# Five coefficient rows of a tile summed in PSUM by products with the identity, instead of by adds on GpSimd

## The chip, the cores and the metric

One core of one Trainium2 chip. The metric is device time in microseconds of one execution. The kernel computes in fp32 on TensorE (matrix products into PSUM), VectorE, ScalarE and GpSimd; SyncE issues the loads and stores. Each engine follows its own list of instructions in order, and they meet at semaphores.

## The reference, cut to what matters

```python
x = x + conv_block(_gn(x))          # 3x3 ternary convolution, 32 channels, 64x64, 16 images
x = x + omp_block(_gn(x))           # sparse coding of 4x4 patches
# omp_block: each patch of 512 numbers is a signal, the dictionary has 256 normalised atoms
for k in range(1, 6):               # five greedy steps for every patch
    index = argmax(|h| of the atoms not yet taken)
    # extend the Cholesky factor, solve for the k coefficients x_stack
    h = h_bar - x_stack @ G[I]
coeffs[b, I] = x_stack              # 5 nonzeros among 256
recon = D @ coeffs
```

For a tile of 128 patches, `coeffs` is a matrix of 128 x 256 with five nonzeros in a row. The kernel makes five matrices with one nonzero per row each, adds them, transposes the sum and multiplies it by the dictionary.

## The kernel before, in words

The 16 images are worked on in ROUNDS = 4 rounds r of IMG_R = 4 images; m counts the image slot. An image has two tiles of 128 patches; a round has two streams s = 0, 1 of TILES = 4 tiles each (two images). In round r the greedy steps k = 0 to 4 run on both streams. Beside them run the front of the next round f = r+1 (statistics, `norm_x`, `conv`, `norm_y`, `correlate`), and the back of the previous one, b = r-1 (coefficients, `reconstruct`, `out_back`, store). Nothing schedules this but the code: each engine's `body(r, front, behind)` calls the pieces in an order written by hand.

A greedy step: ScalarE takes |h| from PSUM into `score` (`scores`, L628). VectorE finds the eight largest and their places (`scan`, L906 and L912), drops those already taken (`select`), and extracts with masks the entries that it needs of the gathered Gram rows and of h (`extract`, `pick`, L964 and L967), then computes the coefficients (`solve`). GpSimd gathers the rows of the Gram matrix by indirect DMA (`gather`, L352), as soon as `select` has given the index. ScalarE builds diagonal matrices of the coefficient steps (`diags`, L637) and TensorE subtracts `diag` times `rows` from h (`update`, through the helper `mm`, L395, as all its ordinary products). VectorE waits for the score before `scan`.

The coefficients of image slot m: VectorE writes for each of its two tiles t five matrices of 128 x 256 into `picked[:, m % 2, t, j, :]`, j = 0 to 4 (`scatter`, L1054), and raises `picked_ready`. GpSimd adds matrices 1 to 4 onto matrix 0, four adds that wait for each other (`sum_picked`, L366), and raises `coef_ready`. TensorE transposes the sum in four blocks of 128 x 128 (`coef_transposes`, L483) into a PSUM tile of 128 x 512 (`back_ps0`, in the closing part `final_ps`, a view of `conv_ps`). ScalarE copies it with its sign turned to `coef_t` (`copy_coef`, L643). `reconstruct` adds, in two halves, x1 (by a product with the identity) and the dictionary times `coef_t`, and ScalarE evacuates each half (`out_back`, L650). `picked` has two places: `scatter` of slot m waits until slot m-2 is transposed.

Slot 0 of round r is scattered in the last selection of the round and slot 1 at its end; slots 2 and 3 have theirs in steps k = 1 and 2 of the next round. GpSimd adds slot 0 at the end of its round, and slots 1, 2 and 3 in the next, behind the gathers of (s, k) = (1, 0), (0, 2) and (0, 3). In TensorE's list `coef_transposes(b, 0)` and `reconstruct(b, 0)` stand between `correlate(r, 1)` and `update(r, 0, 0)`; `coef_transposes(b, 1)` behind `update(r, 0, 1)`; `reconstruct(b, 1)` behind `update(r, 1, 2)`; those of slot 2 behind `update(r, 0, 3)` and those of slot 3 behind `update(r, 1, 3)`, ahead of `correlate(f, 0)`. After the last round comes the closing part: the four images of round 3, one after the other. There VectorE itself adds the second tile of slots 2 and 3 (L1210).

On ScalarE, at the turn of a round: eight activations for the statistics of the next images (`x_statistics`), `scores(r, 1, 0)`, `copy_coef(b, 0)`, `root` (a square root that VectorE's `norm_params` awaits), `diags(r, 0, 0)`, `out_back(b, 0)`, `norm_x(f, 0)`, `scores(r, 0, 1)`, `norm_x(f, 1)`, `diags(r, 1, 0)`. Later `out_back(b, 1)` stands just before `diags(r, 0, 3)`.

Of the kernel before, what the change touches and what calls it, by code (L numbers as in the profile page):

```python
# [27 lines left out]
ALU = mybir.AluOpType  # L28
# [4 lines left out]
def build_program(nc, x_in, w_in, b_in, wc_in, bc_in, gate_in, dict_in, out):  # L33
    IMAGES, C, H, W = x_in.shape
    P = 128
# [5 lines left out]
    STEPS = 5  # L41
    IMG_R = 4
    ROUNDS = IMAGES // IMG_R
    TILES = 4
    CHUNKS = ATOMS // P
# [11 lines left out]
    with ctx:  # L57
# [3 lines left out]
        def sem(name):  # L61
            return ctx.enter_context(nc.semaphore(name))
# [4 lines left out]
        ident = sb("ident", [P, P])  # L67
# [53 lines left out]
        picked = sb("picked", [P, 2, 2, STEPS, ATOMS])  # L121
# [25 lines left out]
        final_ps = conv_ps[:, 0, :].rearrange("p (k n) -> p k n", k=CHUNKS)  # L147
# [47 lines left out]
        diag_ready = [sem(f"diag_ready{s}") for s in range(2)]  # L195
        h_read = [sem(f"h_read{s}") for s in range(2)]
        picked_ready = sem("picked_ready")
        coef_ready = sem("coef_ready")
        coef_ready_dve = sem("coef_ready_dve")
        coef_t_ps = sem("coef_t_ps")  # L200
        coef_t_done = sem("coef_t_done")
        recon_ps = sem("recon_ps")
# [4 lines left out]
        pool_step = sem("pool_step")  # L207
# [15 lines left out]
        def hold(eng, signal, value):  # L223

            eng.wait_ge(signal, value)
# [93 lines left out]
        @block.gpsimd  # L319
        def _(pool):  # L320
            n = 0

            def step(ins):
                nonlocal n
                n += 1
                ins.then_inc(pool_step, 1)
                pool.wait_ge(pool_step, n)

            step(nc.gpsimd.memset(ident[:, :], 0.0))
            step(nc.gpsimd.memset(same_channel[:, :], 0.0))  # L330
            step(nc.gpsimd.memset(center[:, :], 0.0))
            step(nc.gpsimd.memset(ones, 1.0))
            step(nc.gpsimd.iota(iota_i[:, :], pattern=[[1, ATOMS]], base=0, channel_multiplier=0))

            def put_ones(t, offset):

                step(nc.gpsimd.affine_select(out=t, in_=t, compare_op=ALU.not_equal, fill=1.0,
                                             base=-offset, pattern=[[1, t.shape[1]]], channel_multiplier=-1))

            put_ones(ident[:, :], 0)  # L340
            for q in range(1 - PATCH, PATCH):
                put_ones(same_channel[:, :], q * C)
            put_ones(center[:, 0:P // 2], 0)
            put_ones(center[:, P // 2:P], -C)
            step(nc.gpsimd.tensor_copy(iota_short[:, :], iota_i[:, :]))
            nc.gpsimd.tensor_copy(iota[:, :], iota_i[:, :]).then_inc(const_done, 1)

            def gather(r, s, k):

                hold(pool, idx_ready[s], (STEPS - 1) * r + k + 1)  # L350
                for t in range(TILES):
                    pool.indirect_dma_start(out=rows[s][:, k, t, :], out_offset=None, in_=gram_dram[:, :],  # L352
                                            in_offset=bass.IndirectOffsetOnAxis(ap=idx_u[s][:, k, t:t + 1], axis=0)
                                            ).then_inc(rows_in[s][t], 16)

            pool.wait_ge(gram_stored, 16)

            pool_base = n

            def sum_picked(r, m, tiles=(0, 1), left_out=0):  # L360


                for t in tiles:
                    hold(pool, picked_ready, 2 * (IMG_R * r + m) + t + 1)
                    for j in range(1, STEPS):
                        last = nc.gpsimd.tensor_tensor(picked[:, m % 2, t, 0, :], picked[:, m % 2, t, 0, :],  # L366
                                                       picked[:, m % 2, t, j, :], ALU.add)
                        if j < STEPS - 1:
                            count = pool_base + 2 * (STEPS - 2) * (IMG_R * r + m) + (STEPS - 2) * (t - left_out) + j
                            last.then_inc(pool_step, 1)  # L370
                            hold(pool, pool_step, count)
                    last.then_inc(coef_ready, 1)

            def body(r, behind):
                for k in range(STEPS - 1):
                    for s in range(2):
                        gather(r, s, k)

                        if behind and (s, k) in sums_after:
                            sum_picked(r - 1, sums_after[s, k])  # L380
                sum_picked(r, 0)

            sums_after = {(1, 0): 1, (0, 2): 2, (0, 3): 3}
            body(0, False)
            for r in range(1, ROUNDS):
                body(r, True)
            sum_picked(ROUNDS - 1, 1)
            sum_picked(ROUNDS - 1, 2, (0,))
            sum_picked(ROUNDS - 1, 3, (0,), 1)


        @block.tensor
        def _(pe):
# [16 lines left out]
            for c in range(PATCH):  # L410
                last = mm(back_ps[0][:, 0, :], ones, d_tmp[:, c, :], c == 0, c == PATCH - 1)
# [60 lines left out]
            def coef_transposes(r, m, dst=back_ps[0]):  # L472

                n = IMG_R * r + m
                by_dve = m - 1 if dst is final_ps and m >= 2 else 0
                pe.wait_ge(coef_ready, 2 * n + 2 - by_dve)
                if by_dve:
                    pe.wait_ge(coef_ready_dve, by_dve)
                if dst is back_ps[0]:
                    pe.wait_ge(y_done, 2 * n + 2)  # L480
                for k in range(CHUNKS):
                    for t in range(2):
                        last = nc.tensor.transpose(dst[:, k, t * P:(t + 1) * P],  # L483
                                                   picked[:, m % 2, t, 0, k * P:(k + 1) * P], ident[:, :])
                last.then_inc(coef_t_ps, 1)

            def reconstruct(r, m, final=False):
# [285 lines left out]
        def _(dve):  # L773
            v = nc.vector
            n = 0

            def step(ins):

                nonlocal n
                n += 1  # L780
                ins.then_inc(dve_step, 1)
                return n

            def after(count):

                dve.wait_ge(dve_step, count)
# [349 lines left out]
            for m in DVE_SQUARES:  # L1136
                dve.wait_ge(x1_done, 2 * m + 2)
                c = step(v.scalar_tensor_tensor(out=z[:, m, :], in0=x1[:, m, :], scalar=1.0, in1=x1[:, m, :],
                                                op0=ALU.mult, op1=ALU.mult, accum_out=sum_1[:, 2, m:m + 1]))
# [4 lines left out]
            for m in range(IMG_R):  # L1144
                c = step(v.tensor_scalar(z[:, m, :], x1[:, m, :], gn[:, 1, 8, m:m + 1], gn[:, 1, 9, m:m + 1],
                                         ALU.mult, ALU.add))
# [59 lines left out]

            for m in range(2, IMG_R):
                run(scatter(ROUNDS - 1, m))
                for j in range(1, STEPS):
                    c = step(v.tensor_tensor(picked[:, m % 2, 1, 0, :], picked[:, m % 2, 1, 0, :],  # L1210
                                             picked[:, m % 2, 1, j, :], ALU.add))
                    after(c)
                dve.sem_inc(coef_ready_dve, 1)


_INS = ['x', 'L0_conv_w', 'L0_conv_b', 'L0_conv_w_child', 'L0_conv_b_child', 'L0_conv_gate', 'L1_conv_dictionary']
# [18 lines left out]
```

## Time and profile before

| | |
|---|---|
| time, median of 3 runs | 603.63 us (602.96 to 605.72) |
| time of the profiled execution | 602.51 us |
| its span, first to last instruction | 600.7 us |
| TensorE (PE) busy | 457.0 us, 76%, 1778 instructions |
| VectorE (DVE) busy | 523.7 us, 87% |
| ScalarE (ACT) busy | 310.0 us, 52% |
| GpSimd (POOL) busy | 221.4 us, 37%: 127.5 in 128 gathers, 88.9 in 120 adds |
| chain that ended last | DVE 50%, PE 25%, issue 10%, ACT 6% |

The span is what the profiler saw between the first and the last instruction; the time of the execution is measured around it and is a little longer. PEld is TensorE's weight load, which runs beside its products. In a row of a timeline or a group, the last bracket tells how long the engine was idle before, and which instruction ended that.

### The profile page before, as it was taken

The numbers are of one execution on the slowest core, as the hardware profiler recorded it, in microseconds if no ns is written. First come the engines' busy times: TensorE is split into PE (matmuls) and PEld (weight loads), VectorE is DVE, ScalarE is ACT, GpSimd is POOL, SyncE is SP. The second block draws the span as 40 slices with busy tenths as digits, with TensorE's granted clock in tenths as the row PEclk, the third lists the DMA queues.
The fourth block names the chain that finished last, engine by engine and source line by source line (L and its number), as shares of the span: only waits on it lengthen the run. The fifth ranks groups of instructions, "written<-read, shape, count | busy, mean of one in ns | idle before, by whom it ended". The sixth has DMA issues, their size and how long they took to land.

```text
span 600.7 us, 7900 instructions
## 1 busy us (share of the span) xinstructions
PE 457.0 (76%) x1778; PEld 316.9 (53%) x1778; DVE 523.7 (87%) x2507; ACT 310.0 (52%) x682; POOL 221.4 (37%) x269
## 2 busy tenths in 40 slices
PE   0098949897659587889985797999983647896955
PEld 0034935455558343567873444677951535674643
DVE  4493579899999999999999999999999999889980
ACT  3544565785562757665576394658132433452212
POOL 3000045243004665471035656620347475404330
PEclk9999988898888899999998898989995877898868
DMA  6989024987000377651204341121113111211113
GB/s 105 173 114 151 17 60 96 161 124 118 5 1 6 101 130 140 121 102 34 53 19 100 74 97 44 37 71 37 35 47 95 41 50 50 71 35 36 35 35 70
DMA packets 108190, 43.41 MB, mean 72 GB/s; under 512 B 103408, under 2 KB 103920, under 8 KB 108144
## 3 DMA queue, kind: packets, MB, share of 16 engines
q1 hardware_dynamic: 102000, 26.13, 26.5%
q0 software_dynamic: 6144, 16.79, 10.8%
q8 instruction: 14, 0.23, 0.2%
q14 instruction: 32, 0.26, 0.1%
HBM read 34.24 MB, written 8.65 MB: 71 GB/s over the span
## 4 chain that ended last, share of the span: by engine, by line
DVE 50%; PE 25%; issue 10%; ACT 6%; SPq 5%; DMA 3%; POOL 0%; DVEq 0%
PE h L395 14%; DVE picked L1054 11%; DVE junk L967 9%; PE back_ps L395 7%; DVE junk L964 7%; DVE top_i L912 7%; DVE top L906 4%; PE conv_ps L395 4%; SPq L246 3%; ACT diag L637 1%; DVE mask L979 1%; SPq L253 1%; ACT xb L596 1%; ACT xa L596 1%; DMA xb<-in_x 1%
## 5 line engine op out<-in xcount | busy, mean ns | idle before, releaser
L395 PE MATMUL h<-rows,diag 128*128 128x256 f32 x640 | 173.2, 431 | 83.1 <-ACT diag L637 79.2
L352 POOL DMA_INDIRECT rows<-gram,idx_u x128 | 127.5, 996 | 213.5 <-DVEq L952 183.8
L395 PEld LDWEIGHTS h<-rows,diag 128*128 128x128 f32 x640 | 134.9, 217 | 124.2 <-issue 91.5
L366 POOL TENSOR_TENSOR picked<-picked 128x256 f32<-128x256 f32 x120 | 88.9, 744 | 144.9 <-DVEq L1058 137.7
L637 ACT ACTIVATE diag<-ident,dx 128x128 f32<-128x128 f32 x320 | 96.8, 388 | 69.9 <-DVEq L1041 69.8
L628 ACT ACTIVATE score<-h 128x512 f32<-128x512 f32 x80 | 47.2, 595 | 104.9 <-PE h L395 104.9
L1054 DVE TENSOR_SCALAR picked<-iota,idx_last,x_last 128x256 f32<-128x256 f32 x160 | 84.1, 561 | 1.5 <-DVE picked L1054 0.8
L967 DVE SCALAR_TENSOR_TENSOR junk<-mask,rows 128x256 bf16<-128x256 bf16 x224 | 82.4, 429 | 0.1
L906 DVE MAX8 top<-score 128x8 f32<-128x256 f32 x160 | 64.2, 413 | 13.3 <-ACT score L628 12.6
L395 PE MATMUL h<-d_sb,z 128*128 128x256 f32 x256 | 63.0, 407 | 9.0 <-DVEq L897 8.0
L395 PEld LDWEIGHTS h<-d_sb,z 128*128 128x128 f32 x256 | 61.0, 328 | 11.1 <-issue 8.9
L912 DVE FIND_INDEX8 top_i<-top,score 128x8 uint32<-128x256 f32 x160 | 64.9, 417 | 0.0
L395 PE MATMUL back_ps<-coef_t,d_t 128*128 128x256 f32 x256 | 64.1, 395 | 0.0
L395 PE MATMUL back_ps<-x,ident 128*128 128x256 f32 x128 | 63.1, 627 | 0.0
L395 PE MATMUL conv_ps<-xa,w_taps 128*64 128x512 f32 x128 | 62.2, 608 | 1.2 <-ACT x L606 0.8
L395 PEld LDWEIGHTS back_ps<-coef_t,d_t 128*128 128x128 f32 x256 | 51.8, 202 | 21.1 <-issue 14.2
L650 ACT ACTIVATE x<-back_ps 128x512 f32<-128x512 f32 x32 | 33.8, 1094 | 49.3 <-PE back_ps L395 49.3
L395 PE MATMUL conv_ps<-xb,w_taps 128*64 128x512 f32 x112 | 54.5, 610 | 0.0
L964 DVE SCALAR_TENSOR_TENSOR junk<-iota,idx_u,h 128x256 bf16<-128x256 f32 x96 | 44.2, 472 | 1.2 <-DVE idx_u L923 0.6
L964 DVE SCALAR_TENSOR_TENSOR junk<-iota,idx_u,rows 128x256 bf16<-128x256 f32 x96 | 43.4, 512 | 1.8 <-DVE picked L1054 0.7
L395 PEld LDWEIGHTS conv_ps<-xa,w_taps 128*64 128x64 f32 x128 | 16.6, 140 | 35.4 <-issue 33.3
L395 PEld LDWEIGHTS back_ps<-x,ident 128*128 128x128 f32 x128 | 25.6, 208 | 16.3 <-issue 14.6
(148 smaller groups left out, 577.9 us busy)
## 6 DMA issues: line engine op xcount, KB each, us to landing
xa<-in_x SPq DMA_DIRECT2D x64, 128.0 KB, 4.7
out<-x SPq DMA_DIRECT2D x64, 128.0 KB, 2.8
xb<-in_x SPq DMA_DIRECT2D x42, 128.0 KB
rows<-gram,idx_u POOLq DMA_INDIRECT x128, 2.9
xb<-in_x SPq DMA_DIRECT2D x14, 120.0 KB
rows<-in_x SPq DMA_DIRECT2D x6, 128.0 KB, 4.4
d_sb<-in_L_conv_dictionary SPq DMA_DIRECT2D x4, 128.0 KB, 4.0
gram<-coef_t SPq DMA_DIRECT2D x1, 256.0 KB, 2.2
```

The lines of the kernel that those rows point to most:

```text
L246: sp.dma_start(xa[channels(q), m, down:GR + down, 1:W + 1], rows_of(src, q)).then_inc(xa_loaded[m], 16)
L352: pool.indirect_dma_start(out=rows[s][:, k, t, :], out_offset=None, in_=gram_dram[:, :], in_offset=bass.IndirectOffsetOnAxis(ap=idx_u[s][: ...
L366: last = nc.gpsimd.tensor_tensor(picked[:, m % 2, t, 0, :], picked[:, m % 2, t, 0, :], picked[:, m % 2, t, j, :], ALU.add)
L395: return nc.tensor.matmul(dst, lhs, rhs, start=start, stop=stop, skip_group_check=skip)
L628: nc.scalar.activation(score[s][:, 2 * b:2 * b + 2, :], h[s][:, 2 * b:2 * b + 2, :], ACT.Abs).then_inc(score_ready[s], 1)
L637: last = nc.scalar.activation(diag[s][:, t, j, :], ident[:, :], ACT.Copy, scale=dx[s][:, t, j:j + 1])
L650: nc.scalar.activation(dst[:, 2 * half:2 * half + 2, :], back_ps[half][:, :, :], ACT.Copy).then_inc(y_done, 1)
L906: first.append(step(v.max(out=top[s][:, t, :], in_=score[s][:, t, :])))
L912: step(v.max_index(out=top_i[s][:, t, :], in_max=top[s][:, t, :], in_values=score[s][:, t, :]))
L964: c = step(v.scalar_tensor_tensor(out=place, in0=iota[:, :], scalar=idx_u[s][:, k, t:t + 1], in1=source, op0=ALU.is_equal, op1=ALU.mult, a ...
L967: c = step(v.scalar_tensor_tensor(out=place, in0=mask[:, t, :], scalar=1.0, in1=source, op0=ALU.mult, op1=ALU.mult, accum_out=dst))
L1054: c = step(v.tensor_scalar(picked[:, m % 2, t, j, :], iota[:, :], idx_last[m // 2][:, tile, j:j + 1], x_last[m // 2][:, tile, j:j + 1], AL ...
```

## The change

`sum_picked` and its calls go. `coef_transposes` multiplies each of the five matrices of a tile by the identity and lets PSUM accumulate, so that a block's sum comes out transposed; it waits for `picked_ready` of each tile. VectorE's adds in the closing part go as well. Nothing else is changed.

```diff
-            def sum_picked(r, m, tiles=(0, 1), left_out=0):
-                for t in tiles:
-                    hold(pool, picked_ready, 2 * (IMG_R * r + m) + t + 1)
-                    for j in range(1, STEPS):
-                        last = nc.gpsimd.tensor_tensor(picked[:, m % 2, t, 0, :], picked[:, m % 2, t, 0, :],
-                                                       picked[:, m % 2, t, j, :], ALU.add)
...
-                    last.then_inc(coef_ready, 1)
-
-            def body(r, behind):
+            for r in range(ROUNDS):
                 for k in range(STEPS - 1):
                     for s in range(2):
                         gather(r, s, k)
-
-                        if behind and (s, k) in sums_after:
-                            sum_picked(r - 1, sums_after[s, k])
-                sum_picked(r, 0)
...
             def coef_transposes(r, m, dst=back_ps[0]):
                 n = IMG_R * r + m
-                by_dve = m - 1 if dst is final_ps and m >= 2 else 0
-                pe.wait_ge(coef_ready, 2 * n + 2 - by_dve)
-                if by_dve:
-                    pe.wait_ge(coef_ready_dve, by_dve)
                 if dst is back_ps[0]:
                     pe.wait_ge(y_done, 2 * n + 2)
-                for k in range(CHUNKS):
-                    for t in range(2):
-                        last = nc.tensor.transpose(dst[:, k, t * P:(t + 1) * P],
-                                                   picked[:, m % 2, t, 0, k * P:(k + 1) * P], ident[:, :])
+                for t in range(2):
+                    pe.wait_ge(picked_ready, 2 * n + t + 1)
+                    for k in range(CHUNKS):
+                        for j in range(STEPS):
+                            last = mm(dst[:, k, t * P:(t + 1) * P], picked[:, m % 2, t, j, k * P:(k + 1) * P], ident[:, :],
+                                      t == 0 and k == 0 and j == 0, j == STEPS - 1, True)
                 last.then_inc(coef_t_ps, 1)
...
             for m in range(2, IMG_R):
                 run(scatter(ROUNDS - 1, m))
-                for j in range(1, STEPS):
-                    c = step(v.tensor_tensor(picked[:, m % 2, 1, 0, :], picked[:, m % 2, 1, 0, :],
-                                             picked[:, m % 2, 1, j, :], ALU.add))
-                    after(c)
-                dve.sem_inc(coef_ready_dve, 1)
```

On TensorE, from `update(1, 0, 3)` to `reconstruct(1, 0)` at the turn from round 1 to round 2, the order before (a row is a run of like products; `h<-rows,diag` is `update`, `back_ps<-ident,picked` is `coef_transposes`, the two kinds behind it `reconstruct`, `h<-d_sb,z` `correlate`):

```order
178 L395 MATMUL h<-rows,diag 128x256 x16
179 L483 MATMUL back_ps<-ident,picked 128x128 x4
180 L395 MATMUL back_ps<-x,ident 128x256 x2
181 L395 MATMUL back_ps<-coef_t,d_t 128x256 x4
182 L395 MATMUL back_ps<-x,ident 128x256 x2
183 L395 MATMUL back_ps<-coef_t,d_t 128x256 x4
184 L395 MATMUL h<-rows,diag 128x256 x16
185 L483 MATMUL back_ps<-ident,picked 128x128 x4
```

and with the change:

```order
178 L365 MATMUL h<-rows,diag 128x256 x16
179 L365 MATMUL back_ps<-ident,picked 128x128 x20
180 L365 MATMUL back_ps<-x,ident 128x256 x2
181 L365 MATMUL back_ps<-coef_t,d_t 128x256 x4
182 L365 MATMUL back_ps<-x,ident 128x256 x2
183 L365 MATMUL back_ps<-coef_t,d_t 128x256 x4
184 L365 MATMUL h<-rows,diag 128x256 x16
185 L365 MATMUL back_ps<-ident,picked 128x128 x20
```

Twenty ordinary products stand where four transposes stood, at all sixteen places, and no place has moved. On GpSimd, from the first round to the second, the order before is

```order
17 L352 DMA rows<-gram,idx_u 128x256 x32
18 L366 TENSOR_TENSOR picked<-picked 128x256 x8
19 L352 DMA rows<-gram,idx_u 128x256 x8
20 L366 TENSOR_TENSOR picked<-picked 128x256 x8
21 L352 DMA rows<-gram,idx_u 128x256 x12
22 L366 TENSOR_TENSOR picked<-picked 128x256 x8
```

and with the change all 128 gathers follow each other with nothing between:

```order
17 L350 DMA rows<-gram,idx_u 128x256 x128
```

## Rows read from the trace of the kernel before

**Rows 1.** The page, busy time and share of the span of each engine.
```profile
PE 457.0 (76%) x1778; PEld 316.9 (53%) x1778; DVE 523.7 (87%) x2507; ACT 310.0 (52%) x682; POOL 221.4 (37%) x269
```

**Rows 2.** The tile `picked`: instructions, duration ns min/median/max, first and last start.
```profile
L1054 DVE TENSOR_SCALAR picked<-iota,idx_last,x_last x160: 395/406/896, 169.5 to 582.2; 128x256 f32<-128x256 f32 x160
L366 POOL TENSOR_TENSOR picked<-picked x120: 721/727/994, 180.2 to 581.4; 128x256 f32<-128x256 f32 x120
L483 PEld LDWEIGHTS back_ps<-ident,picked x48: 140/141/225, 189.3 to 540.4; 128*128 128x128 f32 x48
```

**Rows 3.** Timeline, 184 to 190 us: start us, us, engine, line, operation.
```profile
184.04 3.14 POOL L366 TENSOR_TENSOR picked<-picked 128x256 f32<-128x256 f32 x4 [0.70 <-DVEq L1058]
184.06 3.60 DVE L1054 TENSOR_SCALAR picked<-iota,idx_last,x_last 128x256 f32<-128x256 f32 x5
...
187.81 1.71 DVE L1054 TENSOR_SCALAR picked<-iota,idx_last,x_last 128x256 f32<-128x256 f32 x5 [0.15 <-DVE picked L1054]
```

**Rows 4.** Stretches: from:to length, busy us of each engine, PEclk, DMA share.
```profile
197.11:320.91 123.80, 105.89 (x436) 73.08 (x435) 119.86 (x597) 78.75 (x174) 55.23 (x64) 0.97 0.43 85
320.91:445.02 124.11, 108.06 (x435) 75.22 (x434) 119.64 (x587) 70.19 (x157) 54.89 (x63) 0.94 0.24 59
445.02:547.85 102.83, 70.25 (x245) 51.20 (x244) 96.52 (x477) 41.91 (x106) 49.24 (x57) 0.82 0.21 56
547.85:594.43 46.58, 34.38 (x112) 24.02 (x112) 34.99 (x98) 10.71 (x12) 16.37 (x23) 0.82 0.20 46
```

**Rows 5.** Timeline of TensorE's products at slot 3 of round 0.
```profile
288.40 0.60 PE L483 MATMUL back_ps<-ident,picked 128*128 128x128 f32 x4
288.84 1.97 PE L395 MATMUL back_ps<-x,ident 128*128 128x256 f32 x4
290.63 1.91 PE L395 MATMUL back_ps<-coef_t,d_t 128*128 128x256 f32 x8
292.38 1.97 PE L395 MATMUL back_ps<-x,ident 128*128 128x256 f32 x4
...
295.92 7.63 PE L395 MATMUL h<-d_sb,z 128*128 128x256 f32 x32
```

**Rows 6.** Weight loads in the views of `w_taps` and `coef_t`, ns min/median/max.
```profile
L395 PEld LDWEIGHTS conv_ps<-xa,w_taps x128: 132/136/232, 33.0 to 375.1; 128*64 128x64 f32 x128
...
L395 PEld LDWEIGHTS back_ps<-coef_t,d_t x256: 187/190/333, 191.2 to 593.8; 128*128 128x128 f32 x128
```

**Rows 7.** Groups of VectorE's instructions, 452.82 to 459.30: busy us, mean ns.
```profile
L1054 DVE TENSOR_SCALAR picked<-iota,idx_last,x_last 128x256 f32<-128x256 f32 x5 | 3.6, 733 | 0.0
L964 DVE SCALAR_TENSOR_TENSOR junk<-iota,idx_u,rows 128x256 bf16<-128x256 f32 x2 | 1.9, 970 | 0.0
```

**Rows 8.** The page, a group of the extractions over the whole span.
```profile
L964 DVE SCALAR_TENSOR_TENSOR junk<-iota,idx_u,h 128x256 bf16<-128x256 f32 x96 | 44.2, 472 | 1.2 <-DVE idx_u L923 0.6
```

**Rows 9.** Timeline of TensorE, four places where it waits in rounds 1 and 2.
```profile
206.44 3.75 PE L395 MATMUL h<-rows,diag 128*128 128x256 f32 x8 [5.96 <-ACT diag L637]
...
267.01 4.34 PE L395 MATMUL h<-rows,diag 128*128 128x256 f32 x19 [2.17 <-ACT diag L637]
...
304.18 7.82 PE L395 MATMUL h<-d_sb,z 128*128 128x256 f32 x32 [0.64 <-DVEq L897]
312.97 0.39 PE L395 MATMUL conv_ps<-sum_x,same_channel 128*128 128x8 f32 x2 [0.97 <-ACT z L581]
```

**Rows 10.** The chain that ended last, at the second half of `out_back(0, 0)`.
```profile
198.42 1.12 ACT x L650
```

**Rows 11.** Timeline of VectorE, third tile of `scan(3, 0, 1)`.
```profile
450.85 0.43 DVE L906 MAX8 top<-score 128x8 f32<-128x256 f32 x1 [0.43 <-ACT score L628]
```

**Rows 12.** Timeline of TensorE, closing part: `coef_transposes` of slots 0 and 2.
```profile
553.45 1.12 PE L483 MATMUL conv_ps<-ident,picked 128*128 128x128 f32 x4 [5.61 <-POOL picked L366]
...
577.21 1.09 PE L483 MATMUL conv_ps<-ident,picked 128*128 128x128 f32 x4 [6.60 <-DVEq L1213]
```

More of the change, by code:

```diff
@@ L197, in build_program @@
         picked_ready = sem("picked_ready")
-        coef_ready = sem("coef_ready")
-        coef_ready_dve = sem("coef_ready_dve")
         coef_t_ps = sem("coef_t_ps")
@@ L356, in _ @@
             pool.wait_ge(gram_stored, 16)
-            pool_base = n
-            def sum_picked(r, m, tiles=(0, 1), left_out=0):
-                for t in tiles:
-                    hold(pool, picked_ready, 2 * (IMG_R * r + m) + t + 1)
-                    for j in range(1, STEPS):
-                        last = nc.gpsimd.tensor_tensor(picked[:, m % 2, t, 0, :], picked[:, m % 2, t, 0, :],
-                                                       picked[:, m % 2, t, j, :], ALU.add)
[L368 to L371, printed above, removed]
-                    last.then_inc(coef_ready, 1)
-            def body(r, behind):
+            for r in range(ROUNDS):
                 for k in range(STEPS - 1):
@@ L377, in body @@
                         gather(r, s, k)
-                        if behind and (s, k) in sums_after:
-                            sum_picked(r - 1, sums_after[s, k])
-                sum_picked(r, 0)
[L383 to L389, printed above, removed]
         @block.tensor
```

## The prediction

> **What bounds the kernel now.** I read the busy shares first [rows 1]: VectorE is busy 87% of the span, TensorE 76%, GpSimd 37%. GpSimd is far from full, so taking 88.9 us of adds from it buys nothing by itself; the question is whom those adds disturb, and whether TensorE has room for what replaces them. Second, the view of the tile `picked` [rows 2]: the scatter instruction of VectorE (L1054) has a median of 406 ns but a maximum of 896. The timeline shows when it is slow [rows 3]: while GpSimd adds, five scatters take 3.60 us (720 ns each); when it has stopped, the next five take 1.71 us. So the two engines shut each other out here. The Trainium skill (SBUF — State Buffer, section "SBUF: two separate sides") says that a VectorE instruction in a two-port mode and a GpSimd instruction hold one port pair exclusively, and the loser blocks; by that rule the trace agrees, 720 ns being about one add's 727 [rows 2].
>
> Third, the stretches. I cut the span at the ends of the three `reconstruct(b, 0)`, of the last `reconstruct` before the closing part and of the last of all: 197.11, 320.91, 445.02, 547.85, 594.43 [rows 4]. In the two stretches of a full round TensorE is busy 105.9 and 108.1 of 124 us, VectorE 119.9 and 119.6: VectorE leads, and TensorE follows with 16 to 18 us of room. That room is what the change spends.
>
> **Step 1, the price of a sum on TensorE.** Now four transposes per image start 0.44 us ahead of what follows, 110 ns each [rows 5]. After, an image takes 20 fp32 products of 128x128 by 128 columns. They aren't transposes, and every ordinary fp32 product shows as two records: `back_ps<-coef_t,d_t` has 4 in the program's order per half, 8 in the trace, at (292.38-290.63)/8 = 219 ns for 256 columns, hence 110 ns for 128 [rows 5]. Is the weight load hidden at that rate? A fp32 load of 64 columns takes 136 ns, of 128 columns 190 [rows 6]; 54 ns for 64 columns is some 107 ns of occupancy for 128, the rest fixed latency that overlaps, as it does for the transposes (loads of 141 ns at a pace of 110 [rows 2, 5]). So load and stream both need about 110 ns and run side by side: 40 records x 0.110 = **4.4 us an image, 3.96 more than now**. No row shows the form itself. The bounds: nothing can stream faster than a transpose's single record, 20 x 0.110 = 2.2 us; and with each load's full 190 ns exposed 40 x 0.190 = 7.6 us. I take 4.4, since its two halves each have a row.
>
> The Trainium skill (TensorE: Matmul & The Clock Gate, section "Terms") calls transpose mode four times faster for fp32. By that rule a product would be 440 ns, an image 8.8 us. The rows make the factor 2 (110 ns against two records of 110), so my sum goes by 2; the factor 4 speaks against this change and is kept as a rival.
>
> **Step 2, what leaves.** 120 GpSimd adds, and 8 adds of VectorE at the end. With them goes the lock-out. Beside the adds of image slot 1, VectorE in 452.82 to 459.30 shows five scatters at 733 ns (against 406) and two extractions at 970 (against 472) [rows 2, 7, 8]: 5x0.33 + 2x0.50 = 2.6 us, with small instructions 3.1. Slot 0 costs twice the 1.89 us that five scatters lose [rows 3], 3.7. For slots 2 and 3, where the adds lie mostly beside instructions that aren't slowed, I estimate half of slot 1's each, 1.5. That is some 10 us a round of VectorE's time, 30 in three rounds, and in the closing part some 13 (five tiles of slowed scatters at 1.89, and 8 adds of its own at about 0.45). It is a true saving of busy time, but it counts only where VectorE still leads.
>
> **Step 3, where it lands.** Against the profiled execution: span 600.7, its own time 602.51; the median of the runs shown is 603.63, 0.2% above it.
>
> - To the first `reconstruct(b, 0)`'s end: `correlate(r, 1)` starts when VectorE has read h, before the adds, so nothing comes earlier, and `coef_transposes(b, 0)` stands before `reconstruct`: **+3.9 us**. VectorE's early 3.6 us end in a wait: ScalarE must copy these coefficients before its square root of the statistics and before `out_back`, `norm_x` and the scores that VectorE wants next.
> - First full stretch, now 123.8. TensorE needs its 105.9 busy [rows 4], plus 4 x 3.96 = 15.8, plus idle time that no engine's spare time removes. First, after `reconstruct(b, 0)` ScalarE evacuates, scores, normalises and builds the diagonals before `update(r, 1, 0)`: 206.44-198.42 = 8.0 us [rows 9, 10], of which `update(r, 0, 0)`, 8 records of 0.219, fills 1.75: 6.3. Second, 2.2 us before `update(r, 0, 3)` [rows 9], whose diagonals queue on ScalarE behind `out_back(b, 1)`. Third, 1.6 us (0.64+0.97) at the end of the round, where ScalarE's eight statistics must finish before the sums. Together 131.8: **+8.0**. VectorE would need 124-10 = 114, so TensorE is now the bound.
> - Second full stretch, now 124.1: the same work at the same clock, without the statistics: 105.9+15.8+6.3+2.2 = 130.2, **+6.1**.
> - Last round, now 102.8, without convolutions: TensorE idles a third of it [rows 4]. The score that VectorE awaited at 450.85, 5.8 us after `reconstruct(b, 0)` [rows 11], comes 2.4 us after it (1.75 of update, 0.6 of score), since the gathered rows have long landed: -3.4. VectorE leads and saves 3.1+1.5. Then `coef_transposes(b, 2)` and `(b, 3)` stand in the path again, +7.9: **-0.1**. What slot 3 saves is lost in the wait for `out_back(b, 1)`, which queues before these diagonals on ScalarE.
> - Closing part, now 46.6, with TensorE idle 5.6 and 6.6 us, awaiting adds of GpSimd and of VectorE [rows 12], and the granted clock 0.82 [rows 4]. These waits vanish: the sums are now late themselves and the scatters early. Four times 4.4 + 7.08 (a `reconstruct`, 288.84 to 295.92 [rows 5]) = 45.9: **-0.7**.
>
> Sum +17.2: span 618, its time **620 us**, 2.8% slower. Everything that the adds cost VectorE is given back as waiting for TensorE, and the closing waits are filled by the new products.
>
> **The rivals.** (A) *The weight load isn't hidden.* At 190 ns a record an image costs 3.2 us more than forecast. Fifteen of the sixteen images lie on the path above (1, 4, 4, 2, 4), so +48: 668 us; with half the latency exposed, 647. By the skill's factor 4 (8.8 us an image, 4.4 more than forecast) +66: 686 us, with 0.03 of this rival's 0.15, for the rows speak for 2. For it: no row has 128 weight columns on 128 moving ones in fp32. Against: in the 256-column form the load is hidden entirely.
> (B) *The products are as cheap as transposes*, one record of 110 ns, 2.2 us an image: 15 x 2.2 = 33 us less than forecast, 587 us, faster than before. It decides at each `coef_transposes`; below about 3.3 us an image (17.2/15 = 1.15 under 4.4) the change is no slower. Against: all ordinary fp32 products come as two records. 0.08.
> (C) *VectorE stays the bound everywhere*, and TensorE's 144 idle us swallow the products: 603.6 less some 40 of lock-out, 563 us. For it: VectorE's 87%. Against: the full stretches leave TensorE 16 to 18 us, 10 of them in waits of TensorE for ScalarE for TensorE that products can't fill. 0.04.
> That the change doesn't do what it says is excluded by the order: 20 products for each 4 transposes, no add left on either engine.
>
> **How the numbers follow.** A measurement of this kernel can tell about 0.5% from no change. Forecast 0.68, its own range 607 to 632 (0.4 us an image on fifteen is 6 us; slow or full clock in three updates 5). Rival A 0.15, B 0.08, C 0.04, and 0.05 that the price lies so between B and mine that nothing shows. Slower 0.83, same 0.05, faster 0.12. The range takes in the half-exposed load at 647 and ends at 606; outside are B, C and the full rival A, about 0.2.
>
> **What would show it.** Right: the products at 110 ns a record, 640 of them; scatters all near 406 ns; VectorE busy near 480 us; the full stretches near 131 us with VectorE waiting for scores at the k=4 scans and at the first scan after `reconstruct(b, 0)`; no idle time of TensorE in the closing part. Wrong in size: a pace of 150 ns or more. Wrong in kind: VectorE still without gaps in the full rounds, or 320 records.

## The result, and the profile after

| | before | changed |
|---|---|---|
| median | 604.67 us (602.96 to 611.05, 4 runs) | 634.68 us (632.05 to 636.88, 4 runs) |
| profiled execution, its span | 602.51, 600.7 us | 633.46, 631.6 us |

The ratio is 1.047, 95% interval 1.039 to 1.056: **slower by 4.7%**, against 2.8% forecast (620 us, range 606 to 647). (The table of the kernel before had three runs; the fourth here is the 611.05.) The changed kernel took 625.2 us in a later set of runs, ratio 1.037 (1.033 to 1.040); the last experiments are about that difference.

The page of the changed kernel, busy times, the shares of the chain that ended last, and two groups (busy us, mean ns of one, idle before):

```profile
PE 517.2 (82%) x2354; PEld 383.3 (61%) x2354; DVE 478.4 (76%) x2499; ACT 312.3 (49%) x682; POOL 134.1 (21%) x149
...
PE 64%; DVE 12%; ACT 8%; issue 5%; SPq 5%; DMA 4%; DVEq 0%; ACTq 0%
...
L874 DVE MAX8 top<-score 128x8 f32<-128x256 f32 x160 | 64.5, 414 | 59.6 <-ACT score L596 58.6
...
L365 PE MATMUL back_ps<-ident,picked 128*128 128x128 f32 x480 | 55.7, 275 | 0.0
```

TensorE and VectorE have changed places [rows 1]: TensorE from 76 to 82%, VectorE from 87 to 76%, and TensorE holds 64% of the chain where it held 25%. VectorE, which before awaited scores for 12.6 us, now awaits them for 58.6.

The tile `picked` in the changed kernel (ns min/median/max, first and last start):

```profile
L365 PEld LDWEIGHTS back_ps<-ident,picked x480: 190/192/207, 190.9 to 571.8; 128*128 128x128 f32 x160
...
L1022 DVE TENSOR_SCALAR picked<-iota,idx_last,x_last x160: 382/407/416, 170.6 to 598.4; 128x256 f32<-128x256 f32 x160
```

No scatter takes 896 ns any more [rows 2]: the longest is 416. The weight load is indeed 190 ns long, as the row of `coef_t` promised [rows 6]. Whether it is hidden shows in TensorE's timeline at the place of [rows 5]:

```profile
298.19 4.63 PE L365 MATMUL back_ps<-ident,picked 128*128 128x128 f32 x40
302.66 1.97 PE L365 MATMUL back_ps<-x,ident 128*128 128x256 f32 x4
```

20 products are 40 records, and they take 302.66-298.19 = 4.47 us, 112 ns each, less than the load's 190: it is hidden. The stretches, cut as before at the ends of `reconstruct(b, 0)`, of the last `reconstruct` of the rounds and of the last of all (columns as in [rows 4]):

```profile
202.83:338.80 135.97, 123.17 (x581) 91.18 (x581) 111.54 (x602) 79.89 (x174) 33.03 (x34) 0.96 0.42 78
338.80:477.43 138.63, 125.39 (x580) 93.64 (x579) 108.54 (x584) 71.06 (x157) 35.17 (x35) 0.93 0.23 58
477.43:579.22 101.79, 78.50 (x355) 63.17 (x354) 88.68 (x467) 40.11 (x101) 24.56 (x24) 0.88 0.18 47
579.22:625.36 46.14, 46.13 (x257) 36.29 (x255) 16.44 (x77) 11.10 (x12) 0.00 (x0) 1.00 0.21 46
```

| change in us | start | first full | second full | last round | closing | sum |
|---|---|---|---|---|---|---|
| forecast | +3.9 | +8.0 | +6.1 | -0.1 | -0.7 | +17.2 |
| this execution | +5.7 | +12.2 | +14.5 | -1.0 | -0.4 | +31.0 |

The excess of 14 us sits in the two full stretches, 12.6 of it. What stands there that the forecast hadn't: first TensorE's wait before `update(1, 0, 2)`. The kernel before had one there as well, of 2.96 us (3.35 in the next round); the forecast didn't keep it:

```profile
239.77 5.42 PE L395 MATMUL h<-rows,diag 128*128 128x256 f32 x24 [2.96 <-ACT diag L637]
```

In the changed kernel, TensorE, and what ScalarE does meanwhile:

```profile
245.62 5.42 PE L365 MATMUL h<-rows,diag 128*128 128x256 f32 x24 [2.38 <-ACT diag L605]
```
```profile
241.68 1.19 ACT L564 ACTIVATE xa<-xa,gn 128x960 f32<-128x960 f32 x1 [1.92 <-DMA xb<-in_x]
...
244.51 3.60 ACT L605 ACTIVATE diag<-ident,dx 128x128 f32<-128x128 f32 x12
```

On ScalarE `norm_x(f, 3)` stands ahead of `diags(r, 0, 2)`. It waits 1.92 us for the load of `xb`, takes 2.9 us, and only then come the diagonals for which TensorE stands still. In the next round the same update is slower as well as late: 7.10 us for the 24 records that took 5.42, at a granted clock of 0.76 over them, so partly at 1.2 GHz instead of 2.4.

```profile
380.26 7.10 PE L365 MATMUL h<-rows,diag 128*128 128x256 f32 x24 [2.42 <-ACT diag L605]
```

This slowness isn't new: in the kernel before the update took 7.10 us too, behind its 3.35 us. The forecast gave the second stretch the 105.9 us of TensorE's time of the first, where [rows 4] has 108.06, and so left it out.

Second, at the turn to round 3, ScalarE's copy of the coefficients:

```profile
469.14 0.60 ACT L611 ACTIVATE coef_t<-back_ps 128x512 f32<-128x512 f32 x1 [7.36 <-remote]
```

The sums that it reads were finished at 465.6, where TensorE went on to the products with x (465.44); the copy starts 3.5 us later with nothing that the trace names in its way ("remote" is a releaser that isn't seen).

### The profile page after: what moved, and what is told of

It reads as the page before. It is cut to its first block, busy times and chain, and to the rows that moved or that the text cites. A ratio compares the mean times of both kernels' runs of the same rounds, so it can differ in the third digit from the quotient of the medians.

```text
span 631.6 us, 8920 instructions
## 1 busy us (share of the span) xinstructions
PE 517.2 (82%) x2354; PEld 383.3 (61%) x2354; DVE 478.4 (76%) x2499; ACT 312.3 (49%) x682; POOL 134.1 (21%) x149
## 4 chain that ended last, share of the span: by engine, by line
PE 64%; DVE 12%; ACT 8%; issue 5%; SPq 5%; DMA 4%; DVEq 0%; ACTq 0%
PE h L365 28%; PE back_ps L365 26%; PE conv_ps L365 11%; DMA xb<-in_x 3%; SPq L244 3%; ACT xb L564 2%; DVE junk L932 2%; DVE top_i L880 2%; ACT diag L605 2%; SPq L251 2%; DVE junk L935 2%; ACT xa L564 1%; DVE picked L1022 1%; DVE top L874 1%; ACT z L549 1%
## 5 line engine op out<-in xcount | busy, mean ns | idle before, releaser
L350 POOL DMA_INDIRECT rows<-gram,idx_u x128 | 129.1, 1009 | 406.5 <-DVEq L920 376.0
L365 PEld LDWEIGHTS h<-rows,diag 128*128 128x128 f32 x640 | 137.8, 219 | 99.2 <-issue 76.6
L874 DVE MAX8 top<-score 128x8 f32<-128x256 f32 x160 | 64.5, 414 | 59.6 <-ACT score L596 58.6
L935 DVE SCALAR_TENSOR_TENSOR junk<-mask,rows 128x256 bf16<-128x256 bf16 x224 | 79.6, 417 | 0.1
L1022 DVE TENSOR_SCALAR picked<-iota,idx_last,x_last 128x256 f32<-128x256 f32 x160 | 59.1, 407 | 3.7 <-PE conv_ps L365 2.4
L365 PE MATMUL back_ps<-ident,picked 128*128 128x128 f32 x480 | 55.7, 275 | 0.0
L365 PEld LDWEIGHTS back_ps<-ident,picked 128*128 128x128 f32 x480 | 55.3, 192 | 0.5
L932 DVE SCALAR_TENSOR_TENSOR junk<-iota,idx_u,rows 128x256 bf16<-128x256 f32 x96 | 40.5, 481 | 1.8 <-DVE picked L1022 0.7
```

The lines of the kernel that those rows point to most:

```text
L365: return nc.tensor.matmul(dst, lhs, rhs, start=start, stop=stop, skip_group_check=skip)
L874: first.append(step(v.max(out=top[s][:, t, :], in_=score[s][:, t, :])))
L932: c = step(v.scalar_tensor_tensor(out=place, in0=iota[:, :], scalar=idx_u[s][:, k, t:t + 1], in1=source, op0=ALU.is_equal, op1=ALU.mult, a ...
L935: c = step(v.scalar_tensor_tensor(out=place, in0=mask[:, t, :], scalar=1.0, in1=source, op0=ALU.mult, op1=ALU.mult, accum_out=dst))
L1022: c = step(v.tensor_scalar(picked[:, m % 2, t, j, :], iota[:, :], idx_last[m // 2][:, tile, j:j + 1], x_last[m // 2][:, tile, j:j + 1], AL ...
```

## Experiments

**Is it VectorE's relief or TensorE's load?** Two kernels do one part of the change each. The first keeps the four transposes and drops the adds:

```diff
-                        for j in range(STEPS):
-                            last = mm(dst[:, k, t * P:(t + 1) * P], picked[:, m % 2, t, j, k * P:(k + 1) * P], ident[:, :],
-                                      t == 0 and k == 0 and j == 0, j == STEPS - 1, True)
+                        last = nc.tensor.transpose(dst[:, k, t * P:(t + 1) * P],
+                                                   picked[:, m % 2, t, 0, k * P:(k + 1) * P], ident[:, :])
```

> The changed kernel with its 20 products per image replaced by the four transposes of before, so that neither engine sums: rows 1 to 4 of each tile are left out of the coefficients. Theory T (TensorE's products cost 4.5 us an image on the path, and the lock-out between GpSimd's adds and VectorE was worth some 35 us to VectorE): without either, VectorE leads again and the time falls below before, to 603 less about 30 (TensorE's waits give some back): 570 to 580 us. Rival G (the adds' lock-out hid behind other waits, and is worth little): 595 to 604 us.

Measured: 569.71 us, ratio 0.945 (0.942 to 0.948). That is just under theory T's range. So the adds with their lock-out and the waits for them had cost 33 us. Its stretches:

```profile
197.10:318.40 121.30, 108.23 (x438) 76.67 (x437) 110.98 (x602) 79.67 (x174) 33.13 (x33) 0.93 0.45 87
318.40:434.10 115.70, 104.42 (x436) 73.31 (x435) 107.32 (x579) 70.63 (x157) 32.12 (x32) 0.97 0.26 64
434.10:528.00 93.90, 69.32 (x247) 52.24 (x245) 85.78 (x462) 39.88 (x101) 28.24 (x28) 0.85 0.22 57
528.00:561.60 33.60, 31.50 (x113) 20.99 (x111) 20.20 (x88) 10.56 (x12) 0.00 (x0) 0.95 0.28 63
```

Against [rows 4] the first full stretch gains 2.5 us, the second 8.4, the last round 8.9 and the closing part 13.0. Even with no product added, VectorE's 9 and 12 us less of busy time in the full stretches don't all become time: TensorE's 104 to 108 us stand right behind. How much of the 20 us outside the closing part is the lock-out and how much is waiting for the sums, these runs don't separate.

The second keeps GpSimd's and VectorE's adds and makes the products too:

```diff
-                for k in range(CHUNKS):
-                    for t in range(2):
-                        last = nc.tensor.transpose(dst[:, k, t * P:(t + 1) * P],
-                                                   picked[:, m % 2, t, 0, k * P:(k + 1) * P], ident[:, :])
+                for t in range(2):
+                    for k in range(CHUNKS):
+                        for j in range(STEPS):
+                            last = mm(dst[:, k, t * P:(t + 1) * P], picked[:, m % 2, t, j, k * P:(k + 1) * P], ident[:, :],
+                                      t == 0 and k == 0 and j == 0, j == STEPS - 1, True)
```

> The kernel before with its adds on GpSimd kept, and the 20 products in place of its four transposes: both the lock-out and the products, and rows 1 to 4 count twice in the coefficients. Theory T (TensorE bounds the changed kernel, so VectorE's saving is wasted there in the full rounds): close to the changed kernel, 634 plus 0 to 8 us. The closing part adds to that, since TensorE waits for the adds again (5.6 and 6.6 us before), so up to 645. Rival G' (the saving of VectorE is already inside the changed kernel's time): the costs add up, 634 plus 30 = 664 us.

Measured: 633.68 us, ratio 1.051 (1.047 to 1.054), within a microsecond of the changed kernel's 634.68, and 8 above its later 625.2. Rival G' is refuted: the costs don't add up. Its second full stretch, and below it the same stretch of that later execution of the changed kernel:

```profile
341.40:475.10 133.70, 122.75 (x579) 90.94 (x578) 117.25 (x584) 71.06 (x157) 58.87 (x68) 0.96 0.24 59
```
```profile
336.20:469.80 133.60, 122.94 (x579) 91.00 (x579) 108.60 (x584) 71.18 (x157) 35.14 (x35) 0.95 0.25 60
```

VectorE is 8.7 us busier with the adds, and the stretch is as long to 0.1 us: in that round they are worth nothing once TensorE leads. The two profiled executions differ elsewhere, in the first full stretch (139.3 against 135.2, of which TensorE's own busy time, at a lower granted clock, is 3.6), in the last round (103.5 against 100.2) and in the closing part (48.7 against 46.1), where TensorE waits for adds again, 1.63 us at the first sum.

**The price of the sum.** The rivals put it anywhere from 2.2 us an image up. Two more kernels vary it. One makes the twenty operations transposes that accumulate:

```diff
-                            last = mm(dst[:, k, t * P:(t + 1) * P], picked[:, m % 2, t, j, k * P:(k + 1) * P], ident[:, :],
-                                      t == 0 and k == 0 and j == 0, j == STEPS - 1, True)
+                            last = nc.tensor.matmul(dst[:, k, t * P:(t + 1) * P], picked[:, m % 2, t, j, k * P:(k + 1) * P], ident[:, :],
+                                      start=t == 0 and k == 0 and j == 0, stop=j == STEPS - 1, is_transpose=True,
+                                      skip_group_check=True)
```

> The changed kernel with its 20 products per image issued as transposes (the transpose mode with the accumulate flags of the products). Theory T: one record of 110 ns each instead of two of 113, 2.2 us an image instead of 4.5, which takes 2.3 x 15 = 35 us off where TensorE leads, down to where VectorE leads again: 598 to 606 us. Whether PSUM accumulates in this mode is open: if it does not, the last row alone is left in the coefficients and the time is the same. Rival P (a transpose costs as much as a product once it accumulates): 634 us. By the Trainium skill's factor of four between fp32 products and transposes a transpose would take 57 ns, and an image 1.1 us.

Measured: 593.14 us (590.54 to 597.36), ratio 0.986 (0.982 to 0.991): 1.4% **faster than before**, by an interval that leaves out no change, though a small step, and 5 us under theory T's range. The coefficients hold the sum of all five rows, so transposes do accumulate in PSUM. TensorE's timeline in its closing part, and the tile `picked`:

```profile
545.26 2.35 PE L451 MATMUL conv_ps<-ident,picked 128*128 128x128 f32 x20
547.45 1.06 PE L365 MATMUL back_ps<-x,ident 128*128 128x256 f32 x2
```
```profile
L451 PEld LDWEIGHTS back_ps<-ident,picked x240: 139/141/231, 189.4 to 538.0; 128*128 128x128 f32 x120
```

A transpose is one record of 110 ns, an ordinary product of the same operands two of 112, and the load is 141 ns instead of 192. The Trainium skill (TensorE: Matmul & The Clock Gate, section "Terms") says a factor of four for fp32 transpose mode; this pair of kernels, which differ in the mode alone, measures 4.47/2.19 = 2.04, and for this shape the measurement decides.

The other one makes 8 products instead of 20 (`for j in range(2)`), between the two in price:

```diff
-                        for j in range(STEPS):
+                        for j in range(2):
...
-                                      t == 0 and k == 0 and j == 0, j == STEPS - 1, True)
+                                      t == 0 and k == 0 and j == 0, j == 1, True)
```

> The changed kernel with the products of rows 0 and 1 alone, 8 an image instead of 20; rows 2 to 4 are left out of the coefficients. Theory T (what counts is TensorE's time for a sum): 16 records of 0.113 = 1.8 us an image, a little less than the 20 accumulating transposes (2.2 us, 593.1), so 587 to 592 us. Rival I (the products cost more than their time, by the clock or the length of the list): 598 to 610 us.

Measured: 585.74 us, ratio 0.969 (0.963 to 0.974), a little below the first range there and far below the rival's. It is TensorE's time for the sum that counts, not that it is made of products:

| an image's sum on TensorE, us | time, us | slope from the row above |
|---|---|---|
| 0.44 (4 transposes) | 569.7 | |
| 1.8 (8 products, 16 records of 0.112) | 585.7 | 0.74 |
| 2.2 (20 transposes) | 593.1 | 1.2 |
| 4.5 (20 products) | 625.2 | 0.87 |

The slope is the time gained over the TensorE time added in sixteen images, for instance (625.2-593.1)/(16 x 2.3) = 0.87. (The step of 0.4 is too short for its 1.2 to mean much. The rows are from different sets of runs, in which the kernel before took 602.6 to 604.1 us; the last is the set without the late copy.) A microsecond on TensorE is paid for three quarters or more, from the first one on. By the last slope, 14 us of time for each microsecond an image, 603.6 is reached 10.5 us above the transposes' time, at 2.2 + 10.5/14 = 2.9 us an image.

**Can the new load be put into TensorE's waits?** Two edits of the changed kernel, each in one engine's order. In the first, `coef_transposes(b, 1)` goes into the wait before `update(r, 1, 0)`:

```diff
                 update(r, 0, 0)
+                if behind:
+                    coef_transposes(b, 1)
                 update(r, 1, 0)
...
                 update(r, 0, 1)
-                if behind:
-                    coef_transposes(b, 1)
```

> The changed kernel with the products of image slot 1 put ahead of update(r, 1, 0), where TensorE waits 6.3 us for ScalarE's diagonals, instead of behind update(r, 0, 1). Theory T: the 4.5 us fall into the wait in both full rounds, and that update no longer runs its first records at 1.2 GHz (it took 3.75 us for 8 records where 1.9 is full speed): 4.5 to 6 us less in each, 622 to 626 us. Rival W (the time behind the price is a chain of waits through ScalarE and the loads, not TensorE's work): within 3 us of the changed kernel, 631 to 637 us.

Measured: 619.34 us, ratio 1.028 (1.024 to 1.032). `update(1, 1, 0)`, first in the changed kernel, then in this one:

```profile
210.86 3.75 PE L365 MATMUL h<-rows,diag 128*128 128x256 f32 x8 [6.30 <-ACT diag L605]
```
```profile
210.35 1.97 PE L365 MATMUL h<-rows,diag 128*128 128x256 f32 x8 [1.82 <-ACT diag L605]
```

The wait falls from 6.30 to 1.82 us, and the eight records behind it from 3.75 to 1.97 us: the granted clock over them is 0.50 (1.2 GHz) behind 6.30 us of idleness, and 1.00 (2.4 GHz) behind 4.6 us of products and 1.82 of idleness. The full stretches are 132.5 and 130.2 us, against 135.2 and 133.6 in the later execution of the changed kernel. Not all of the clock's gain is kept: `update(1, 0, 2)` now takes 6.98 us for its 24 records, against 5.42 in that execution.

The second edit, on ScalarE, takes the missed wait away:

```diff
+                diags(r, 0, 2)
                 if front:
                     norm_x(f, 3)
-                diags(r, 0, 2)
```

> The changed kernel with one step of ScalarE's list moved: diags(r, 0, 2) ahead of norm_x(f, 3). In the changed kernel TensorE waits 2.4 us before update(r, 0, 2) in both full rounds, behind a load into xb that can start only when conv(f, 1) has ended, and runs that update partly at 1.2 GHz. Theory L (this chain conv, load, norm_x, diagonals is part of what the forecast missed): the wait goes, 2.4 us and up to 1.7 of clock in each of the two rounds, 5 to 8 us less, 626 to 630 us. Rival V (the diagonals come late anyway, from VectorE): within 2 us of the changed kernel, 633 to 637.

Measured: 618.91 us, ratio 1.027 (1.023 to 1.030). ScalarE and TensorE at the same place:

```profile
239.14 3.62 ACT L605 ACTIVATE diag<-ident,dx 128x128 f32<-128x128 f32 x12 [0.45 <-DVEq L1009]
```
```profile
242.26 5.45 PE L365 MATMUL h<-rows,diag 128*128 128x256 f32 x24
```

TensorE no longer waits there. The full stretches are 131.6 and 129.9 us, 3.6 and 3.7 less than in that later execution: the waits, 2.0 and 2.2 us, and some 1.5 us of TensorE's busy time in each (121.14 for 122.75, 121.48 for 122.94). In the first stretch that is the clock of `update(1, 0, 3)`, first in the changed kernel's later execution, then in this one:

```profile
268.48 8.82 PE L365 MATMUL h<-rows,diag 128*128 128x256 f32 x32 [2.17 <-ACT diag L605]
```
```profile
267.75 7.14 PE L365 MATMUL h<-rows,diag 128*128 128x256 f32 x32 [2.17 <-ACT diag L605]
```

Behind the same wait of 2.17 us, the granted clock is 0.50 over that update's first 2.0 us there, and 1.00 throughout here, where TensorE had not stood still before `update(1, 0, 2)`.

Both results lie below the ranges, which were taken from 634.7. Neither profile has the late copy, so they are to be held against the 625.2 us without it, and there each edit is worth 6 us; the 15 seen against 634.7 aren't theirs. Both together:

> The changed kernel, with the ordinary products, and both moves: slot 1's products ahead of update(r, 1, 0) and diags(r, 0, 2) ahead of norm_x(f, 3). Theory T with L (two separate waits of TensorE on the path): each move is worth some 7 us in the profiles, both together 12 to 14 less than the changed kernel on the same chip: 612 to 615 us beside 626, or 620 to 623 beside 634. Rival O (they take away the same wait): no better than either alone, 617 to 620.

Measured: 617.84 us, ratio 1.023 (1.021 to 1.026), no better than either. ScalarE and TensorE show why:

```profile
237.47 3.61 ACT L605 ACTIVATE diag<-ident,dx 128x128 f32<-128x128 f32 x12 [5.10 <-DVEq L1009]
```
```profile
238.60 3.63 PE L365 MATMUL h<-rows,diag 128*128 128x256 f32 x9 [2.59 <-ACT diag L605]
```

So it came out as rival O said. With the sum gone from the stretch between, TensorE arrives some 5 us sooner, 35.2 us after the end of `reconstruct(0, 0)` (236.0-200.8) instead of 40.0 (241.0-201.0), and now VectorE's coefficients are last: a wait of 2.6 us again, with another cause. The first edit alone already shows it: there `norm_x(f, 3)` starts at 233.79 without waiting, the diagonals wait 2.27 us for VectorE and TensorE 2.59 us for them, so that the second edit had no wait of its own left to remove. That was the cause before the change too, as ScalarE in the kernel before shows:

```profile
233.09 1.18 ACT L596 ACTIVATE xa<-xa,gn 128x960 f32<-128x960 f32 x1
...
238.64 1.57 ACT L637 ACTIVATE diag<-ident,dx 128x128 f32<-128x128 f32 x5 [2.64 <-DVEq L1041]
```

There `norm_x` waited for nothing: its load had been issued at 227.50 and was in by 233.09, 5.6 us later. In the changed kernel it was issued at 234.34 and used at 241.68, 7.3 us later. What makes it longer isn't shown.

**The same edits on the cheap form.** Accumulating transposes with the first move:

> The accumulating transposes (593.1 us) together with those of slot 1 moved ahead of update(r, 1, 0), where TensorE waits 6 us. Theory T: TensorE still bounds part of the full rounds, so 2.2 us go from the path in each and the slow records of update(r, 1, 0) with them: 585 to 590 us. Rival F (with cheap sums VectorE leads there and the place doesn't matter): 592 to 595 us.

Measured: 589.34 us, ratio 0.979 (0.976 to 0.982), in theory T's range. With both moves:

> Accumulating transposes, those of slot 1 moved, and diags(r, 0, 2) ahead of norm_x(f, 3). Theory L: 2 to 4 us under the kernel with the first two alone, 582 to 587 us; the floor is the kernel without any sum, 569.7. Rival V: the same as with the first two alone.

Measured: 588.43 us, ratio 0.977 (0.974 to 0.980), the fastest that makes the whole sum: 2.3% faster than before, 5.9% than the changed kernel's 625.2. The second move adds nothing here that can be told from no change, as rival V said.

**Why 634 here and 625 there?** The changed kernel was run again, unedited, three times.

> The changed kernel once more, for a second profile. In the first, ScalarE copied the coefficients at the turn to round 3 3.4 us late with all its inputs there, and TensorE waited 2.4 us and ran slow behind it. If that belongs to the kernel (its list of instructions is longer), the wait stands at the same place again and the time is 632 to 637 us; if it is chance, it is gone or elsewhere and the stretch from reconstruct(1, 0)'s end to reconstruct(2, 0)'s end takes 134 us instead of 138.6.

Measured: 626.31 us, one execution, second full stretch 134.0, no late copy.

> The changed kernel timed again in five rounds. Its first runs gave 632 to 637 us, a later single one 626.3 without the late copy at the turn to round 3. Theory C (chance: a late copy of some 4.6 us, or two, falls into some executions and not into others): the runs spread from 625 to 637, the median near 630. Rival K (it belongs to the kernel, and the single run was the exception): all of them again at 632 to 637.

Measured: 634.12 us (631.41 to 638.67, 6 runs), ratio 1.051 (1.045 to 1.057); as rival K said; the copy is late again at the same place, idle 8.8 us before it, and starts 5.0 us after the sums were finished.

> The changed kernel a third time, on the chip of the next run. Two sets of runs gave medians of 634.7 and 634.1 us with, in both profiles, ScalarE's copy late by 3.4 to 5 us at the turn to round 3; a single run on the chip that timed the kernel with the diagonals first gave 626.3 without it. Theory C2 (the late copy comes and goes with the chip or the session): on a chip without it 625 to 628 us, on one with it 632 to 637, all runs of a set alike. Rival K (the single 626.3 was the exception): 632 to 637 everywhere.

Measured: 625.18 us (624.20 to 627.67, 4 runs), ratio 1.037 (1.033 to 1.040), which refutes rival K. The copy at the turn to round 3, and the stretches:

```profile
462.75 0.60 ACT L611 ACTIVATE coef_t<-back_ps 128x512 f32<-128x512 f32 x1 [3.87 <-PE back_ps L365]
```
```profile
201.01:336.20 135.19, 122.75 (x582) 91.15 (x581) 110.65 (x599) 79.95 (x174) 32.53 (x33) 0.96 0.42 78
...
469.80:570.00 100.20, 76.90 (x354) 61.98 (x354) 88.59 (x467) 40.11 (x101) 24.95 (x24) 0.90 0.18 48
570.00:616.14 46.14, 46.14 (x257) 36.30 (x255) 16.46 (x77) 11.10 (x12) 0.00 (x0) 1.00 0.21 46
```

Of four profiles, the two from sets at 634 have the late copy and the two at 625 to 626 haven't. The late copy goes with the slower time, but by itself it isn't all of it. In the first execution it costs some 3.6 us: TensorE waits 2.4 and is 1.3 slower behind it (8.3 us from the copy's start to the end of `reconstruct(2, 0)`, against 7.0). Between this execution and the first, the second full stretch differs by 5.0 us, the start by 1.8, the first full stretch by 0.8, the last round by 1.6. e8 and e9 ran on the same chip, so the chip alone doesn't decide. Within the second full stretch 1.7 of the 5.0 us are `update(2, 0, 2)`, 7.10 us there and 5.42 here. What makes the copy late, and what the rest is, stays open; no run here took it apart.

## Why the prediction came out as it did

**The direction and its reason were right.** That GpSimd's load buys nothing by itself, that the adds cost through VectorE's lock-out, and that all of it is given back because TensorE's full stretches have too little room: e1 and e2 show this, except that no run separates the lock-out from the waiting for the sums. The Trainium skill's rule on the shared port pair (SBUF — State Buffer, section "SBUF: two separate sides") agrees with the scatters, at most 416 ns without the adds, and up to 897 again in e2 with them; that it is the port pair which locks, no run here shows. VectorE's busy time came to 478.4 against some 480 forecast.

**The number fell inside the range partly by luck.** The sum said 620 us and gave its own mechanism 607 to 632; the 634.7 is outside that, and inside the whole range only because its upper end, 647, was put at a half-exposed weight load, which didn't occur. (The working there is off, too: half of rival A's 48 us is 24, which makes 644.) The later 625.2 us lies inside 607 to 632.

**Step 1, the price**, is confirmed: 640 records, 112 ns each for 110. The 0.08 us an image by which it was short make 1.3 us in all. Rival A fell with it. Rival B is refuted for this kernel, and e5 gives what it would have been: 593 us where it said 587. Its threshold was slightly high too, 2.9 us an image against 3.3.

**Step 2, what leaves**, was 43 us of VectorE's time by the forecast (30 in the rounds, 13 at the end); its busy time fell by 523.7-478.4 = 45.3. That rival C would have made 563 of it was close as well: e1, which is that case all but in name, gave 570.

**Step 3 is where the sum was short**, in its terms for the full stretches. The clean comparison is e11, whose sum is 622.4-600.7 = +21.7 against +17.2:

- *Start*: +3.9, exact by luck. The other three executions of the same kernel have +4.6, +5.3 and +5.7.
- *Full stretches*: 135.2 and 133.6 against 131.8 and 130.2, so 3.4 short in each. Of that TensorE's busy time is 1.1 and 1.2 (122.75 and 122.94 against 105.9+15.8 = 121.7), and idle time the rest. The prediction counted three waits (6.3, 2.2, 1.6) as idle time "that no engine's spare time removes", and put a fourth at nothing without saying why: the one before `update(r, 0, 2)`, 2.96 and 3.35 us in the trace of before. There the diagonals on ScalarE had awaited VectorE, which the change relieves; but next in line stood `norm_x(f, 3)` with its load, and 2.0 and 2.2 us of waiting were left. e3 removes them and the slow clock that followed, and its stretches of 131.6 and 129.9 us are the forecast's 131.8 and 130.2: the missed term accounts for the whole shortfall there.
- *Last round*: 100.2 against 102.7. Without any sum it is 8.9 us shorter than before (e1), where the forecast's terms make 8.0; the sums bring it back up by 6.3 us (93.9 to 100.2), where the forecast has 7.9. These 2.5 us too many hid a part of the 6.8 too few above.
- *Closing part*: 46.1 against 45.9, with TensorE busy all 46.14 us of 46.14, as forecast; each of its sums is 4.5 for 4.4.

Of the remaining 9 us of the first comparison some 3.6 are the late copy and 1.7 the slow `update(2, 0, 2)`; the rest has no cause shown. No step of the forecast rested on the copy. The waits of VectorE came where they were forecast, 3.4 us at the first scan after `reconstruct(0, 0)` and 4.2 after `reconstruct(1, 0)`, and in late scans of the round, but also at two places in the middle.

## What to carry to other kernels

Work that moves from an engine which is nearly never the last to one which is within 15% of the bound is paid there nearly in full (0.74 to 0.87 of it here): read the room of each stretch, less the waits that are made of third engines, and compare it with the new load before counting what is saved. When a wait in the old trace is ended by the engine that the change relieves, look one instruction further up the releasing engine's queue for what is next in line; it can take over. And where an identity product only turns a block round, ask for transpose mode: for these fp32 blocks of 128 x 128 it halved the price, and it still accumulated.

## What the runs showed of the hardware

- Transposes accumulate in PSUM with start and stop flags as products do: 20 an image in e5, at 110 ns, one record each.
- An ordinary fp32 product of 128 weight columns on 128 moving ones is two records with a load of 192 ns, yet runs at 112 ns a record, so the loads are hidden; TensorE held this for the whole closing part at granted clock 1.00.
- After a wait of 6.3 us eight records took 3.75 us, at a granted clock of 0.50 (1.2 GHz); after one of 1.8 us behind 4.6 us of products 1.97 us, at 1.00 (2.4 GHz). So filling a wait with work can pay a second time behind it: e3, by removing a wait, gained 1.7 us of clock at the update behind the next one, while e4 lost 1.6 of its 1.8 us again at `update(1, 0, 2)`, behind its next wait.
- ScalarE's copy began 3.5 and 5.0 us after its operand was finished, in two of four profiles of one kernel and at the same instruction. It is unexplained.
